# Graph network layers in one kernel: count products in two halves with the row adds between the head products, and eight one-hots in one instruction

## The reference, cut to what matters

```python
def gat_layer(x, W, a_s, a_d, b, src, dst):          # twice, H = 4 heads of C = 32
    h = (x @ W).reshape(-1, H, C)
    e = leaky_relu(al_src[src] + al_dst[dst], 0.2)
    w = exp(e - segment_max(e, dst)[dst])
    alpha = w / maximum(segment_sum(w, dst)[dst], 1e-16)
    return segment_sum(h[src] * alpha[:, :, None], dst).reshape(-1, H * C) + b
...
m = relu(concat([x[src], edge_emb_W[edge_type]]) @ msg_W.T + msg_b)   # the last layer
agg = segment_sum(m, dst) / clip(deg, 1)
```

## Time and profile before

| what | value |
|---|---|
| median of 3 runs | 6585.06 us (6582.29 to 6586.45) |
| the profiled execution | 6585.18 us |
| its span, first to last instruction | 6583.4 us |
| TensorE busy, matmuls | 3267.9 us |
| VectorE busy | 3229.1 us |
| ScalarE busy | 1838.9 us |
| POOL busy | 3503.1 us |
| attention sweep, layer 0: first to last count product starts | 2371.7 to 3050.1 us |
| attention sweep, layer 1: last count product starts | 4244.8 us |
| gathers of the last layer | 5500.4 to 6516.9 us |

### The profile page before, as it was taken

One profiled execution on the slowest core, in us unless ns is written; L12 is line 12 of the kernel. 1 busy time (PEld: TensorE's weight loads), 2 busy tenths in 40 slices (PEclk: granted clock), 3 DMA queues, 4 the chain that ended last, 5 costly groups with the idle time before them and its releaser, 6 DMA issues.

```text
span 6583.4 us, 57054 instructions
## 1 busy us (share of the span) xinstructions
PE 3267.9 (50%) x14965; PEld 1809.5 (27%) x14966; DVE 3229.1 (49%) x4162; ACT 1838.9 (28%) x2842; POOL 3503.1 (53%) x2602
## 2 busy tenths in 40 slices
PE   1311111111116557765334676698899872444444
PEld 0211111111112222222332222244444442333333
DVE  4455555444439977785997787701111124111112
ACT  0100000000014457776444777610011132000001
POOL 0477777777778888888888500000000004777774
PEclk5555555555557777777556777799999985555555
DMA  9322122222239822222993222266655535222222
GB/s 413 97 0 0 0 0 1 1 1 1 1 78 350 291 70 71 80 63 85 312 309 106 70 78 62 62 249 252 239 185 202 197 124 171 52 52 52 52 52 42
DMA packets 341559, 744.34 MB, mean 113 GB/s; under 512 B 170495, under 2 KB 247913, under 8 KB 301925
## 3 DMA queue, kind: packets, MB, share of 16 engines
q1 hardware_dynamic: 171504, 686.10, 29.7%
q0 software_dynamic: 163840, 54.71, 8.9%
q10 hardware_dynamic: 6146, 2.68, 0.2%
HBM read 549.51 MB, written 187.36 MB: 112 GB/s over the span
## 4 chain that ended last, share of the span: by engine, by line
PE 24%; issue 21%; DVE 14%; DMA 14%; POOL 13%; ACT 8%; SPq 1%; POOLq 1%; DVEq 0%; ACTq 0%
PE PS L605 22%; POOL edge_weight_and_count L552 11%; DVE tiles L1381 5%; DMA tiles<-message_table,gather_index 5%; DMA edge_weight_and_count<-weight_and_count,target 4%; DVE feature_major L1305 4%; DMA tiles<-edge_weight_and_count 3%; POOL tiles L583 2%; ACT tiles L1012 2%; ACT tiles L1018 2%; ACT PS L1005 1%; PE PS L706 1%; DVE tiles L1363 1%; PE PS L630 1%; DMA message_table<-tiles 1%
## 5 line engine op out<-in xcount | busy, mean ns | idle before, releaser
L583 POOL DMA_INDIRECT tiles<-message_table,gather_index x808 | 771.3, 955 | 2012.0 <-DMA message_table<-tiles 1765.9
L552 POOL DMA_INDIRECT edge_weight_and_count<-weight_and_count,target x784 | 1241.0, 1583 | 684.6 <-issue 250.6
L572 POOL DMA_INDIRECT sorted_edges<-record_slot,place_slot x784 | 1304.9, 1664 | 298.2 <-issue 216.4
L605 PE MATMUL PS<-tiles 128*64 128x392 f32 (+1 forms) x3200 | 797.9, 658 | 251.3 <-DVE tiles L1381 232.2
L1381 DVE SCALAR_TENSOR_TENSOR tiles<-tiles,copies_then_records 128x3136 f32<-128x3136 f32 (+1 forms) x200 | 684.6, 3423 | 283.6 <-ACT tiles L1018 277.3
L605 PE MATMUL PS<-tiles,stationary_tile 128*128 128x448 f32 (+1 forms) x2100 | 808.9, 548 | 22.3 <-ACT stationary_tile L911 22.2
L861 PE MATMUL PS<-tiles 128*128 128x128 f32 x1616 | 491.7, 460 | 609.3 <-DMA tiles<-message_table,gather_index 609.3
L1305 DVE SCALAR_TENSOR_TENSOR feature_major<-tiles,s,feature_major 128x1600 f32<-128x1600 f32 (+3 forms) x384 | 679.7, 1845 | 41.6 <-ACT tiles L969 41.5
L1460 DVE TENSOR_TENSOR tiles<-lane_row,edges 128x256 f32<-128x256 f32 x404 | 171.7, 426 | 850.9 <-PE PS L861 850.9
L861 PEld LDWEIGHTS PS<-tiles 128*128 128x128 f32 x1616 | 374.7, 322 | 726.8 <-issue 726.8
L605 PEld LDWEIGHTS PS<-tiles,stationary_tile 128*128 128x128 f32 (+1 forms) x2100 | 404.9, 193 | 423.6 <-issue 398.8
(11 more groups left out here) (223 smaller groups left out, 3867.8 us busy)
## 6 DMA issues: line engine op xcount, KB each, us to landing
tiles<-edge_weight_turned SPq DMA_DIRECT2D x72, 1568.0 KB, 7.6
tiles<-edge_count SPq DMA_DIRECT2D x72, 1568.0 KB, 7.3
tiles<-edge_weight_and_count SPq DMA_DIRECT2D x48, 1600.0 KB, 8.9
edge_weight_and_count<-tiles SPq DMA_DIRECT2D x48, 1568.0 KB, 38.7
copies_then_records<-edge_count SPq DMA_DIRECT2D x192, 392.0 KB
tiles<-edge_weight_and_count SPq DMA_DIRECT2D x48, 1536.0 KB
edge_weight_turned<-copies_then_records SPq DMA_DIRECT2D x48, 768.0 KB
edge_count<-copies_then_records SPq DMA_DIRECT2D x24, 800.0 KB, 4.6
```

The costliest lines, as they stand in the source:

```text
L552: nc.gpsimd.indirect_dma_start(out=edge_d, out_offset=bass.IndirectOffsetOnAxis(ap=idx[:, s, a:a + 1], axis=0), in_=pay[:, s, a, :], in_of ...
L572: nc.gpsimd.indirect_dma_start(out=rec_d, out_offset=bass.IndirectOffsetOnAxis(ap=place_slot[:, s, a:a + 1], axis=0), in_=rec_slot[:, s, a ...
L583: nc.gpsimd.indirect_dma_start(out=msg[:, s, a, :], out_offset=None, in_=table_d, in_offset=bass.IndirectOffsetOnAxis(ap=gs[:, s, a:a + 1] ...
L605: return nc.tensor.matmul(out_ap, lhsT, rhs, start=start, stop=stop)
```

## The change

In the attention step the count product is split by head pair: half 0 (heads 0 and 1, 128 x 1568) as soon as E0, E1 and the count block are there, then the logits of t+1, then half 1. w_made counts two a tile. TensorE's row adds are taken apart and set between the head products. ScalarE's tile becomes E0, E1, K0, D2, K1, D3, feature copy, and the copy of the sums moves from tile 1 to tile 0. In the gather stage one VectorE instruction makes the one-hots of a whole turn (128 x 1024) into one of three blocks (HOT = 8 chunks each), which lie where table tile 0 was; VectorE's 101 instructions are written out, TensorE's loop has three turns in its body.

```diff
-        hot = tiles[0:TP, 2 * TN * D:2 * TN * D + 4 * GM * TP].rearrange("p (s b n) -> p s b n", s=4, b=GM)
+        hot = tiles[0:TP, 0:3 * HOT * TP].rearrange("p (s b n) -> p s b n", s=3, b=HOT)
...
 # SyncE, before a block's load
-                        sp.wait_ge(S("w_made"), t + (base + 1))
+                        sp.wait_ge(S("w_made"), t * 2 + (2 * base + 2))
...
 # TensorE
-                def attend(m, t, c):
+                def attend(m, t, c, g):
...
-                    pe.wait_ge(S("hp_made"), t + (NT * m + 1))
-                    pe.wait_ge(S("w_made"), t + (NT * m + 3))
+                    if g == 0:
+                        pe.wait_ge(S("hp_made"), t + (NT * m + 1))
+                    pe.wait_ge(S("w_made"), t * 2 + (2 * NT * m + g + 5))
...
-                            add_row(m, t + 1)
...
-                        attend(m, t, c)
+                        for g in range(2):
+                            if ahead:
+                                add_row(*to, g)
+                            attend(m, t, c, g)
...
 # TensorE, gather stage, one turn; the loop's body has three
+            def sum_block(i, block):
+                pe.wait_ge(S("lanes_made"), i * 1 + 1)
...
-                    pe.wait_ge(S("lanes_made"), i * 4 + (s + 1))
...
 # ScalarE
                         exp_e(m, t, c, 0)
+                        exp_e(m, t, c, 1)
+                        if ahead:
+                            kink(*to, 0)
                         exp_d(m, t, c, 2)
                         if ahead:
-                            kink(*to, 0)
-                        if isinstance(t, int) and t == 1 and q:
+                            kink(*to, 1)
+                        if isinstance(t, int) and t == 0 and q:
                             copy_sums(q - 1)
-                        exp_e(m, t, c, 1)
                         exp_d(m, t, c, 3)
-                        if ahead:
-                            kink(*to, 1)
                         copy_features(m, t, c)
...
 # VectorE
+                def weigh(g, t, c):
+                    n = rows_of(t)
+                    part = U[c % 3][0:n, 2 * g:2 * g + 2, :]
+                    v.scalar_tensor_tensor(part, part, 1.0, B[c % 2][0:n, :].unsqueeze(1).to_broadcast([n, 2, AW]),
+                                           ALU.min, ALU.mult).then_inc(S("w_made"), 1)
...
+                        dve.wait_ge(S("exp_e"), t * 2 + (2 * NT * m + 4))
+                        dve.wait_ge(S(f"block_in{c % 2}"), (k * 3 + c // 2) * 16 + 16)
+                        weigh(0, t, c)
...
                         dve.wait_ge(S("exp_made"), t * 2 + (2 * NT * m + 2))
...
+                        weigh(1, t, c)
...
 # VectorE, gather stage
+            dve.wait_ge(S("table_out0"), 16 * ((TYPES + 2) // 3))
+            for i in range(TURNS):
+                if i >= 3:
+                    dve.wait_ge(S("messages_summed"), 4 * (i - 2))
+                v.tensor_tensor(hot[:, i % 3, :, :], lane_row[:, :].unsqueeze(1).to_broadcast([TP, HOT, TP]),
+                                lane[:, group(i, HOT)].unsqueeze(2).to_broadcast([TP, HOT, TP]), ALU.is_equal).then_inc(S("lanes_made"), 1)
```

More of the change, by code:

```diff
@@ L44 @@
 TURNS = NCH // (4 * GM)
+HOT = 4 * GM
 TW, TN = 112, 28
@@ L764, in _, with add_row @@
                 last.then_inc(S("smax_turned"), 1)
-                def add_row(m, t):
+                def add_row(m, t, h):
                     n = rows_of(t)
[L770 to L775, removed]
@@ L777, in attend @@
-                def attend(m, t, c):
-                    first, stop = isinstance(t, int) and t == 0, isinstance(t, int) and t == NT - 1
-                    pe.wait_ge(S("hp_made"), t + (NT * m + 1))
-                    pe.wait_ge(S("w_made"), t + (NT * m + 3))
-                    n = rows_of(t)
[L782 to L789, removed]
+                    pe.wait_ge(S("kink_made"), t * 2 + (2 * NT * m + h + 1))
@@ new lines, in add_row @@
+                    for u in range(2):
+                        last = nc.tensor.matmul(kinks[h][0:n, u, :], ones_b[0:3, 0:n], parts[m % 2][:, h, u * AH:(u + 1) * AH],
+                                                start=False, stop=True, skip_group_check=True)
+                    last.then_inc(S("row_added"), 1)
+                def attend(m, t, c, g):
+                    first, stop = isinstance(t, int) and t == 0, isinstance(t, int) and t == NT - 1
+                    if g == 0:
+                        pe.wait_ge(S("hp_made"), t + (NT * m + 1))
+                    pe.wait_ge(S("w_made"), t * 2 + (2 * NT * m + g + 5))
+                    if m and first:
+                        pe.wait_ge(S("sums_copied"), 2 * m + g - 1)
+                    n = rows_of(t)
+                    for u in range(2):
+                        for e in range(2):
+                            last = mm(acc[g][u][64 * e:64 * e + 64], hp[c % 2][0:n, g, 64 * e:64 * e + 64],
+                                      U[c % 3][0:n, 2 * g + e, u * AH:(u + 1) * AH], first, stop)
+                    if g:
+                        last.then_inc(S("hp_free"), 1)
@@ L797, in _ @@
                 first_m = AQ * layer
-                add_row(first_m, 0)
+                for h in range(2):
+                    add_row(first_m, 0, h)
                 for q in range(AQ):
@@ L802, in body @@
                     def body(t, c, k):
-                        if not (isinstance(t, int) and t == NT - 1):
-                            add_row(m, t + 1)
-                        elif q + 1 < AQ:
+                        last = isinstance(t, int) and t == NT - 1
+                        to = (m + 1, 0) if last else (m, t + 1)
+                        ahead = not last or q + 1 < AQ
+                        if last and ahead:
                             pe.wait_ge(S(f"rows_in{(q + 1) % 2}"), 16 * 3 * (2 * layer + (q + 1) // 2 + 1))
-                            add_row(m + 1, 0)
-                        attend(m, t, c)
+                        for g in range(2):
+                            if ahead:
+                                add_row(*to, g)
+                            attend(m, t, c, g)
                     sweep6(pe, m, body)
@@ L852, in _ @@
             pe.wait_ge(S("tiles_made"), 1)
-            with pe.Fori(0, TURNS) as i:
+            def sum_block(i, block):
+                pe.wait_ge(S("lanes_made"), i * 1 + 1)
                 _, at = nc.values_load_multi_w_load_instructions(
@@ L858, in _ @@
                     pe.wait_ge(S(f"gathered{s}"), i * (16 * GM) + 16 * GM)
-                    pe.wait_ge(S("lanes_made"), i * 4 + (s + 1))
                     for a in range(GM):
-                        last = nc.tensor.matmul(flat[:, bass.ds(at[s * GM + a], TP)], msg[:, s, a, :], hot[:, s, a, :],
+                        last = nc.tensor.matmul(flat[:, bass.ds(at[s * GM + a], TP)], msg[:, s, a, :], hot[:, block, s * GM + a, :],
                                                 start=False, stop=False, skip_group_check=True)
                     last.then_inc(S("messages_summed"), 1)
+            with pe.Fori(0, TURNS // 3) as i:
+                for block in range(3):
+                    sum_block(i * 3 + block, block)
+            for block in range(TURNS % 3):
+                sum_block(TURNS // 3 * 3 + block, block)
             product([(adel, P0)], [("agg_scaled", 1)], "upd_out")
```

21 lines of the change are left out of this document (3 added, 18 removed).

## The result

| kernel | median | lowest to highest | runs |
|---|---|---|---|
| before | 6583.68 us | 6580.02 to 6586.45 | 4 |
| changed | 6732.02 us | 6711.90 to 6739.84 | 4 |

The ratio is 1.0221, with a 95% interval of 1.0198 to 1.0244. Forecast were 6633 us with a range of 6570 to 6690: the direction is right, the size is three times what was said, and the time lies outside the range.

What follows compares the result with a forecast made beforehand. No engine was full; a ring closing every second tile paced attention, POOL the gathers. Attention 1352 + 35 clock + 22 ends = 1409 against 1371, +38; gather +10; 6585 + 48 = 6633 us, range 6570 to 6690.

Steps and rivals of the forecast that it cites:

- The ring of one tile: Attention sweeps: feature copy, head products 0, row add 1, exponential 1, four more ScalarE operations to next copy; 6.76 us a tile.
- What a long tile costs: Attention tile at 1.2 GHz: slower half products and row add cost about 1.4 us more.
- One tile in eight at the low clock: Attention sweeps: 25 tiles meet 1.2 GHz at 1.4 us each, adding 35 us.
- The bound of one in three: Attention sweeps: upper bound on tiles meeting the low clock, 67 x 1.4 = 94 us.
- The clock's mean: Attention sweeps: sign of a right forecast, TensorE's mean clock rising from 0.75 to over 0.9.
- Quarter ends: Sweeps: moved copy of the sums 1.5 plus VectorE's combining 2.1, 3.6 us for each of 6 ends, 22 us.
- VectorE's half product: Attention sweeps: each half of VectorE's count product takes 1.79 us.
- VectorE's 5.4 us a tile as the pace without a ring: Rival for the sweeps: no ring exists and VectorE's 5.4 us bounds each tile; no chance of its own.
- Count blocks: Attention sweeps: the count block's transfer stays hidden, needed 8.1 us after issue; a four times larger one takes 7.3.
- Gather stage: Gathers held by longer one-hots: 8 us over 98 turns plus 2 at the head, +10 us.
- The nearest rival: Attention sweeps: one tile in three meets the low clock, since a slow tile lengthens the next gap; 6692 us, chance 0.12.

Runs made afterwards that it cites:

- The two cuts of the ring, at either joint: Changed kernel with ScalarE's feature copy right behind exponential 1: 6350.10 us, ratio 0.9664; changed kernel with both row adds ahead of the head products: 6304.37 us, 0.9579.
- the kernel with zeros: Changed kernel with three products of zeros between row add 0 and head products 0 of every tile but each quarter's first: 6591.84 us, ratio 1.0020.

## Why the prediction was wrong in size

Going by its own steps:

- **The ring of one tile**: right. Forecast 6.76, ends 6.65 and 6.85. The turn shown above is 6.69, the short intervals average 6.62 and 6.67. Of its terms, the copy's hand-over was 0.13 as said, the half products 1.47 for 1.44, and ScalarE's five operations and the copy 4.46 for 4.45. The row add with its hand-over was 0.63 for 0.74: ScalarE starts 0.13 behind it, not 0.24. The two cuts of the ring, at either joint, confirm that it is a ring. The sum was 22 us too high here (13.5 in layer 0 and 8.6 in layer 1, for 100 tiles each).
- **What a long tile costs**: somewhat low, 1.68 measured for 1.4 (the forecast's own figures, 2.6 for 1.44 and 0.83 for 0.50, give 1.5). The half products take 2.81 where 2.6 was taken: the 5.09 us of before, which was halved for it, was not all at the low level (mean clock 0.60 in the earlier trace rows). The row add's 0.32 is as said.
- **One tile in eight at the low clock**: this is the step that failed. 50 of the 93 intervals of layer 0 that touch no quarter's first or last tile are long, one in two, and they average 8.29 against 6.62 us: 50 x 1.66 = 83 us. In layer 1 it is 50 again, 8.30 against 6.67, 81 us. That is 164 in both, where the sum had 35. (Three of the 50 also hold the combining of tile 22; against that, two long ones at quarter ends are left out.) The bound of one in three was no bound either. The reason given, that the gap of 2.5 us is half of that before, looked at the gap alone, and at what makes the clock fall, never at what makes it rise. What the trace shows is that the level lasts: of layer 0's 55 long intervals 52 stand in runs of three to five, and of its 44 short ones 34 in runs of four or five. The clock falls in a gap of 2.31 us like those before it that cost nothing, and it stays low over a stretch in which TensorE is busy 28.40 of 33 us. In before each long run of work (5.66 of 5.70 us) was followed by one short tile: the two alternated one by one, and the forecast priced single tiles, as if each fall cost one. What raises the clock again, and why it lasts here, no run isolates; that the level lasts and what it costs is all that they show.
- **The clock's mean**: 0.73 instead of over 0.9. It had been named as what would show the forecast wrong ("a clock that stays near 0.75").
- **Quarter ends**: right in the total by luck, since its two parts are off in opposite directions. At each of layer 0's three ends there is one interval of 9.62 us, with the zeros in the gap as without them, 3.0 over the short ones (1.5 forecast). The combining in tile 22 makes 8.85 and 5.61, or 8.81, 5.30 and 6.13, in the kernel with zeros, where the neighbours are short: 1.2 and 0.4 over the short ones (2.1 forecast). Together 3.4 to 4.2 for 3.6.
- **VectorE's half product** 1.79: measured 1773 to 1864 ns, 1789 in the median. VectorE's 5.4 us a tile as the pace without a ring (it was added up with 1.75 for the 1.79): 5.30 in the steady tiles of the kernels that cut it, 5.33 to 5.46 as the mean of all that are not long. "No chance of its own", the forecast said of this rival, and in the changed kernel that held.
- **Count blocks**: hidden, as said. VectorE waited for one once in the sweep, 5.2 us at its very start.
- **Gather stage**: +3.1 for +10. The one-hot takes 1226 ns for 1.22 us, and the head costs its 2 us (0.98 + 0.98). The steady state gave 1 us in place of 8. In the turn shown the one-hot starts 0.17 behind a gather and ends 0.14 into the next, which ends 0.83 behind it, all as taken (0.15 to 0.28, 0.11 to 0.24, 0.82); of the forecast's 0 to 0.1 us a turn the lower end was the true one.

By the corrected terms the sum is 38 + 129 for the clock - 22 for the ring + 1 for the ends = 146 us for attention, against 147.8 measured in the two sweeps. The direction, too, hangs on the clock: without its 164 us the same terms give an estimate of 18 us less than before for attention, where the forecast had 3 more. The nearest rival was that of one tile in three, 6692 us at 0.12, whose mechanism ("a slow tile lengthens the next gap") isn't the one seen: in the ring at 1.2 GHz the gap is shorter, 1.15 us for 2.31.

## What to carry to other kernels

When two instructions change places, follow each wait in a circle through the queues back to itself before counting anybody's busy time: here one feature copy that stood last, behind a row add set between two products, cost over 6% of the kernel (1.0221 against 0.9579) beside the same change with the adds ahead. Where TensorE works half of each short period, read the granted clock in stretches of several tiles, and price the low level as a level that lasts for tiles, not as a price of single ones. If such a gap can't be closed, products of zeros in it are a cheap test of what the clock is worth, and sometimes a remedy.

## What the runs showed of the hardware that was not expected

- The clock keeps either level over several tiles of the same instructions: four short and five long ones in the stretch shown. TensorE was busy for a larger share of the stretch at 1.2 GHz (28.40 of 33 us) than of the one at 2.4 (17.18 of 29), with the same instructions in each tile, and yet the clock stayed low from 2798.58 to 2834.85.
- 0.92 us of zeros in each tile raised the mean clock from 0.73 to 0.93; 12 instructions a tile of the same kind raised that of before from 0.75 to 0.96 and made it 2.6% faster. Nothing but zeros was multiplied in either.
- An indirect DMA that starts while VectorE compares two SBUF operands is held until about 0.85 us behind that instruction: 1.93 us for 0.96. The Trainium skill (SBUF — State Buffer, Who interferes with whom) says both that a VectorE instruction with two SBUF inputs contends with a GpSimd one that reads SBUF, and that tensor_tensor did not stall descriptor generation; the two held gathers and the 1971 ns of the gather stage alone speak for the first, and against the second.
- Between two chips the gather stage differed by some 145 us with the old one-hots (1016.5 and 1016.8 us on the first, 1161.6 to 1164.7 on the second) and by 139 with the new ones (1019.6 in the changed kernel, 1158.4 with the gather stage alone changed), with the median gather the same to 2 ns. With the new ones POOL's gathers were busy 805.0 us for 774.6, and its idle time inside the stage was 354.3 us (2150.7 less 1796.4 in the row below) for 245.9 (2377.0 less 2131.1), most of the difference waits for TensorE's products (54.7) and for signals from elsewhere (22.7). Why is open.

```profile
L583 POOL DMA_INDIRECT tiles<-message_table,gather_index x808 | 805.0, 996 | 2150.7 <-DMA message_table<-tiles 1796.4 <-issue 271.2 <-PE PS L862 54.7
```
